# Local attention of a hybrid layer one stage earlier: key sums in global attention, values in the mixing stage, routing at its end

## What is computed

```python
# 1. local attention (windows of 2x2 pixels, 256 windows an image) and a convolutional MLP
q, kv = xw @ wq.T * gq + bq, xw @ wkv.T * gkv + bkv
logit = q_win * SCALE @ k_win.T                 # window means
r_idx = top_k(logit, 4)                         # routing: four windows for each window
k_sel, v_sel = kv[r_idx]                        # 16 keys, 8 heads of 16 channels
x = x + softmax(q * SCALE @ k_sel) @ v_sel + dwconv5x5(v_img, w_lepe) + b_lepe
x = x + fc2(relu(dwconv3x3(fc1(x))))
# 2. global attention over the 1024 tokens of an image, 4 heads of 32 channels
t = t + attention(layernorm(t))
# 3. mixture of experts: 8 experts of 128x128, two chosen for each token
n = layernorm(t); t = t + n + sum_e(combine[:, e] * (gelu(n @ w1[e] + b1[e]) @ w2[e] + b2[e]))
```

## Time and profile before

| | us |
|---|---|
| median of 3 runs | 2374.11 |
| lowest and highest run | 2373.70, 2374.38 |
| the profiled execution's own time | 2376.31 |
| its span, first to last instruction | 2374.8 |

### The profile page before, as it was taken

How to read it: one execution, slowest core, us unless ns; L and a number is a source line. 1 busy time by engine, 2 the same in 40 slices (tenths; PEclk the granted TensorE clock), 3 DMA queues, 4 the chain that set the end, 5 groups by cost and what they waited for, 6 DMA issues and landing times.

```text
span 2374.8 us, 39761 instructions
## 1 busy us (share of the span) xinstructions
PE 1640.0 (69%) x15168; PEld 1067.5 (45%) x15168; DVE 1498.8 (63%) x2500; ACT 940.0 (40%) x1285; POOL 1130.7 (48%) x582
## 2 busy tenths in 40 slices
PE   2006457876687856777568874787667885889897
PEld 1003235644455534545346543564345543555565
DVE  2992686548774486736766378653877548852654
ACT  0001235523464315632256233552245522753682
POOL 1994893248803595046930389114880349600000
PEclk9558768987889878889789897888878987999998
DMA  4102000100002000020000100011000200000000
GB/s 148 45 0 98 10 0 19 58 34 0 10 19 81 10 1 10 19 81 10 10 19 15 68 9 10 19 47 44 0 10 19 72 10 0 10 1 2 10 2 10
DMA packets 26138, 61.75 MB, mean 26 GB/s; under 512 B 4192, under 2 KB 13408, under 8 KB 25824
## 3 DMA queue, kind: packets, MB, share of 16 engines
q0 software_dynamic: 9216, 33.56, 4.1%
q1 hardware_dynamic: 16736, 25.60, 3.3%
HBM read 46.56 MB, written 12.58 MB: 25 GB/s over the span
## 4 chain that ended last, share of the span: by engine, by line
PE 35%; DVE 31%; issue 20%; POOL 7%; ACT 5%; DVEq 1%; SPq 1%; DMA 1%; POOLq 0%; ACTq 0%
PE psB L371 8%; PE psB L487 6%; DVE PROD L921 5%; POOL KV L1253 5%; DVE KVSEL L928 5%; PE psB L452 5%; DVE PT L1123 4%; DVE P L1010 4%; PE psA L538 4%; PE psB L507 3%; DVE STACKED L1110 2%; PE psB L435 2%; POOL KVSEL L1240 2%; PE psB L504 2%; ACT P L675 1%
## 5 line engine op out<-in xcount | busy, mean ns | idle before, releaser
L1271 POOL TENSOR_TENSOR XLEPE<-XLEPE,KVSEL 128x1024 f32<-128x1024 f32 x175 | 430.9, 2462 | 14.6
L1010 DVE CUSTOM_DVE_ANT_0 P<-psB,W 128x1024 f32<-128x1024 f32 x256 | 312.9, 1222 | 132.2 <-PE psB L371 105.1
L1253 POOL TENSOR_TENSOR KV<-KVSEL,Q 128x1024 f32<-128x1024 f32 x112 | 262.1, 2369 | 234.1 <-DVE S L897 189.7
L1240 POOL DMA_INDIRECT KVSEL<-window_table,CHOSEN x64 | 60.9, 952 | 621.1 <-DVEq L968 533.5
L675 ACT ACTIVATE P<-P,NEGMAX 128x1024 f32<-128x1024 f32 x256 | 292.8, 1144 | 157.5 <-DVE NEGMAX L1013 154.9
L487 PE MATMUL psB<-W,P 128*128 128x128 f32 x2048 | 317.8, 305 | 53.1 <-DVE NEGMAX L1010 33.6
L683 ACT ACTIVATE PT<-psB 128x1024 f32<-128x1024 f32 x256 | 260.9, 1019 | 145.6 <-PE psB L487 141.4
L487 PEld LDWEIGHTS psB<-W,P 128*128 128x128 f32 x2048 | 258.7, 155 | 124.8 <-issue 86.1
L371 PE MATMUL psB<-STACKED 96*128 96x512 f32 x512 | 213.2, 502 | 131.9 <-DVE NEGMAX L1010 110.8
L1267 POOL TENSOR_SCALAR KVSEL<-V_PAD,W 128x1024 f32<-128x1024 f32 x175 | 255.3, 1459 | 54.1 <-POOL XLEPE L1271 34.6
L1123 DVE SCALAR_TENSOR_TENSOR PT<-psB,PT 128x128 f32<-128x128 f32 x512 | 137.9, 342 | 218.2 <-PE psB L507 213.4
(11 more groups left out here) (128 smaller groups left out, 2277.1 us busy)
## 6 DMA issues: line engine op xcount, KB each, us to landing
window_table<-KV SPq DMA_DIRECT2D x8, 1024.0 KB, 4.0
X<-x_by_window_dram SPq DMA_DIRECT2D x8, 512.0 KB, 3.5
XLEPE<-x_dram SPq DMA_DIRECT2D x8, 512.0 KB, 3.5
out_dram<-PT SPq DMA_DIRECT2D x8, 512.0 KB, 4.6
W<-packed_dram SPq DMA_DIRECT2D x1, 3714.5 KB, 11.7
KVSEL<-window_table,CHOSEN POOLq DMA_INDIRECT x64, 5.7
FC<-packed_dram SPq DMA_DIRECT2D x8, 64.0 KB, 2.4
PROD<-gains_dram SPq DMA_DIRECT2D x1, 256.0 KB, 12.3
```

Source lines behind the costliest of these rows:

```text
L1010: dve.tensor_tensor_reduce(P[:, b, :], ps[:], w("band", at, at + TOK), 1.0, -3.0e38, ALU.mult, ALU.max, NEGMAX[:, b, 0:1]).then_inc(free, 1)
L1253: pool.tensor_tensor(PRODUCTS[i % 2].rearrange("p (k c) -> p k c", c=C), KVSEL[:, t, keys, 0:C], Q[:, t, q, :].unsqueeze(1).broadcast_to([ ...
L1271: pool.tensor_tensor(acc, acc, product, ALU.add).then_inc(lepe_done, 1)
```

## The change

The local attention is pipelined one stage deeper. `attention(n)` now begins with the residual of image n+1 and then runs the 16 key sums and four softmax steps of image n+2, one at each of 20 of the 31 units. `mixing(n)` runs the 16 value steps of image n+2, ten of them ahead of `accumulate(0)`, and ends with the routing of image n+3. On PE the routing's matmuls leave the attention part of the table for experts 4 to 7, and the transposes of attended values move from the start of the mixing stage to behind experts 1 and 2. The residual writes its sum to TN instead of in place, so that XLEPE is free for the next raster image at once; RT, which had lain in TN, gets its own tile. ACT loses one of seven function table loads an image. SP issues the raster load ahead of the table store. The loop runs over images 0 to 4. Ahead of it, image 1's key sums and softmax run before the first mixing stage, and that stage has its 16 value steps and the routing of image 2.

```diff
@@ -100,12 +102,13 @@
 
 def mixing_order():
 
-    order = [("var", 1, 0), ("wo", 1), ("rstd", 1, 0), ("centred", 1, 1), "image values", ("fc1", 0), ("var", 1, 1), ("fc1", 1),
-             ("rstd", 1, 1), "router", ("dw", 0, 0), ("dw", 0, 1), ("hidden", 0), ("fc1", 2), "start", "combine",
-             ("hidden", 1), ("fc1", 3), ("dw", 1, 0), ("dw", 1, 1)]
+    order = [("var", 1, 0), ("wo", 1), ("fc1", 0), ("rstd", 1, 0), ("centred", 1, 1), ("fc1", 1), ("var", 1, 1),
+             ("dw", 0, 0), ("dw", 0, 1), ("rstd", 1, 1), ("fc1", 2), "router", ("hidden", 0), ("fc1", 3), "start", "combine",
+             ("hidden", 1), ("dw", 1, 0), ("dw", 1, 1)]
     beside = {0: ["fc2"], 1: [("centred", 0, 0), ("centred", 0, 1)], 2: [("var", 0, 0), ("var", 0, 1)],
-              3: [("rstd", 0, 0), ("rstd", 0, 1)], 4: ["v", ("q", 0), ("k", 0)], 5: [("q", 1), ("k", 1)],
-              6: [("q", 2), ("k", 2), ("scores", 0)], 7: [("q", 3), ("k", 3)]}
+              3: [("rstd", 0, 0), ("rstd", 0, 1)], 4: ["windows", "v", ("q", 0), ("k", 0), "logits"],
+              5: [("rows", 0), ("q", 1), ("k", 1), ("rows", 1)],
+              6: [("rows", 2), ("q", 2), ("k", 2), ("rows", 3), ("scores", 0)], 7: ["image values", ("q", 3), ("k", 3)]}
     for e in range(EXPERTS):
         order.append(("expert", e))
...
 
 ORDER_B = main_order()
-RING_B = Ring([(name, m) for m in range(2) for name in ROUTING + ["image values"]]
-              + [(name, 0) for name in ORDER_B if images_ahead(name) == 1], ORDER_B, images_ahead, 3)
+RING_B = Ring([(name, m) for m in range(2) for name in ROUTING + ["image values"]], ORDER_B, images_ahead, 3)
 RING_A = Ring([(("attended", t), 0) for t in range(WTILES)],
               [("pv", c) for c in range(TT)] + [("attended", t) for t in range(WTILES)], images_ahead, 2)
...
-EARLY_STEPS = 28
-EARLY_LINKS = 14
-
-WINDOW_STEPS_AT = [4, 7, 11, 14, 17, 20, 23, 27]
+SCORE_STEPS = 20
+VALUE_LINKS = 22
+
+SCORE_STEPS_AT = [1, 2, 3, 4, 5, 7, 8, 9, 10, 12, 13, 14, 15, 17, 18, 19, 21, 23, 26, 28]
 LINKS_B = 67 - 4 - TT
 LINKS_FIRST = 13
 
...
@@ -226,7 +227,7 @@
         NEGMAX = sb("NEGMAX", [128, P_BUFFERS, 2])
         L = sb("L", [128, TT, HEADS_C])
 
-        RT = TN[:, HALF + 2 * C:HALF + 3 * C]
+        RT = sb("RT", [128, 128])[:]
         ACC = PT[:, GROUPS]
 
...
             def load_raster(m):
                 if not (isinstance(m, int) and m == 0):
-                    sp.wait_ge(x2_ready, 2 * (2 * m - 1))
+                    sp.wait_ge(x1_ready, m)
                 sp.dma_start(XLEPE[:], x[bass.ds(m, 1)].rearrange("a c n -> (a c) n")).then_inc(raster_in, 16)
 
...
                 sp.dma_start(out[bass.ds(n, 1)].rearrange("a (t p) c -> p (a t) c", p=128), ACC).then_inc(out_done, 16)
 
-            def image_traffic(n, first, after):
+            def image_traffic(n, first, third, after):
 
                 if first is not None:
-                    store_table(first)
+                    load_raster(first)
+                if third is not None:
+                    store_table(third)
                 if after is not None:
                     x_is_free(after)
                     load_x(after)
-                if first is not None:
-                    load_raster(first)
                 store_out(n)
 
...
+                if images[2] is not None and name in (("expert", 1), ("expert", 2)):
+                    a_attended(images[2], name[1] - 1)
+
+            def image(n, second, first, third):
 
...
                         exp(u + 1, n)
                     turned(u, n)
-                    if first is not None and ROUTED_AT.get(u) == "windows":
-                        a_windows(first)
+                    if first is not None and u in (SCORE_STEPS_AT[16], SCORE_STEPS_AT[17]):
...
+                if third is not None:
+                    a_values(third)
+                if second is not None:
+                    high(3, second)
 
             act.wait_ge(weights_in, 16 * WEIGHT_DMAS)
...
                 for p in range(PX):
                     hy, wx = divmod(p, 2)
-                    place = XLEPE[:].rearrange("c (j hy i wx) -> c hy j i wx", **dims)[:, hy, 8 * t:8 * t + 8, :, wx]
+                    place, summed = (x[:].rearrange("c (j hy i wx) -> c hy j i wx", **dims)[:, hy, 8 * t:8 * t + 8, :, wx]
+                                     for x in (XLEPE, TN))
                     second_chain(m).mark(dve.scalar_tensor_tensor(
-                        out=place, in0=psA[s][:, p * 128:(p + 1) * 128].rearrange("c (j i) -> c j i", j=8),
+                        out=summed, in0=psA[s][:, p * 128:(p + 1) * 128].rearrange("c (j i) -> c j i", j=8),
                         scalar=col("b_lepe"), in1=place, op0=ALU.add, op1=ALU.add))
...
                 steps = []
                 if second is not None:
-                    later_chain.at_image(second - 1, EARLY_LINKS)
-                    steps = second_half(second)[EARLY_STEPS:]
-                front = first_half(first) if first is not None else []
-                run(front, 1)
+                    later_chain.at_image(second - 1, VALUE_LINKS)
+                    for t in range(WTILES):
+                        window_residual(second, t)
+                if first is not None:
+                    later_chain.at_image(first - 1)
+                    steps = second_half(first)[:SCORE_STEPS]
                 for u in range(1, UNITS):
                     scale_scores(u, n)
...
                 for half in range(2):
                     chain.link(dve.scalar_tensor_tensor(out=XR[:, columns(half)], in0=ps[:, columns(half)], scalar=col("b_fc2"),
-                                                        in1=XLEPE[:, columns(half)], op0=ALU.add, op1=ALU.add))
+                                                        in1=TN[:, columns(half)], op0=ALU.add, op1=ALU.add))
                     dve.sem_inc(x2_ready, 1)
...
                     dve.sem_inc(out_ready, 1)
 
-            def mixing(n, second, first, chain):
-                steps = []
-                if first is not None:
-                    steps = second_half(first)[:EARLY_STEPS]
+            def mixing(n, second, first, third, chain):
+                steps = second_half(first)[SCORE_STEPS:] if first is not None else []
+                front = first_half(third) if third is not None else []
                 if n is not None:
                     spread(1, 0, n)
                     projected(1, n)
-                    if second is not None:
-                        for t in range(WTILES):
-                            window_residual(second, t)
+                    run(steps, 2)
                     normalise(1, 0, n, chain)
                     spread(1, 1, n)
                     dve.tensor_tensor(XR[:, columns(0)], XR[:, columns(0)], LATER_TN[0], ALU.add).then_inc(sum_ready, 1)
+                    run(steps, 2)
                     normalise(1, 1, n, chain)
                     dve.tensor_tensor(XR[:, columns(1)], XR[:, columns(1)], LATER_TN[1], ALU.add).then_inc(sum_ready, 1)
-                if first is not None:
-                    later_chain.at_image(first - 1)
-                run(steps, 2)
-                if n is not None:
+                    run(steps, 2)
                     experts_chosen(n, steps)
                 run(steps, 2)
                 accumulate(0, n)
-                run(steps, 3)
+                run(steps, 2)
                 if second is not None:
                     fc2_residual(second, chain)
-                run(steps, 3)
+                run(steps, 2)
                 accumulate(1, n)
-                run(steps, 3)
+                run(steps, 16)
                 accumulate(2, n)
-                run(steps, 3)
+                run(front, 1)
                 if second is not None:
                     for half in range(2):
                         spread(0, half, second)
                 accumulate(3, n)
-                run(steps, 2)
                 if second is not None:
                     for half in range(2):
                         normalise(0, half, second, chain)
-                run(steps, 2)
                 accumulate(4, n)
                 if second is not None:
                     values(second, chain)
                     low(0, second, chain)
+                run(front, 1)
                 accumulate(5, n)
-                run(steps, 4)
+                run(front, 1)
                 if second is not None:
                     low(1, second, chain)
+                run(front, 1)
                 accumulate(6, n)
-                run(steps, 2)
+                run(front, 1)
                 if second is not None:
                     low(2, second, chain)
+                run(front, 1)
+                if second is not None:
                     scale_scores(0, second)
                 accumulate(7, n)
-                run(steps, 4)
                 if second is not None:
                     low(3, second, chain)
                     chain.check()
```

(16 more changed lines are left out.)

113 lines of the change are left out of this document (58 added, 55 removed).

## The result

| | before | after |
|---|---|---|
| median, us | 2374.24 (4 runs) | 2280.25 (4 runs) |
| lowest and highest run, us | 2373.70, 2377.97 | 2267.83, 2292.22 |
| the profiled execution's own time, us | 2376.31 | 2267.83 |
| its span, us | 2374.8 | 2265.6 |
| mean granted TensorE clock | 0.841 | 0.855 |

The ratio is 0.960, with a 95% interval of 0.955 to 0.966: 94 us faster, where 2291 had been predicted, which is 83 us. The profiled execution of after happens to be its fastest, so its stages sum to 12 us less than the median.

The account below looks back on a forecast made before the run. No engine alone bounds; PE and DVE hand over to each other. Start +55, attention 0 to 5 -91, mixing 0 to 4 -15, mixing 5 -14, attention 6 -18: -83, so 2291 us, range 2220 to 2365.

Parts of the forecast that it names:

- The hole takes the value steps: Mixing ahead of accumulate(0): 38 us of value steps cost 13; mixing's parts become 77, 39 and 48 us.
- Rival A: Mixing: value steps are not hidden, accumulate(0) comes 14 us later than forecast, total 2429 us; chance 0.10.
- Blocking: Mixing ahead of accumulate(0): nine short DVE operations beside POOL's taps lose 8 us, bounds 0 and 25 us.
- the 7.5 us of a pair: Mixing, value steps beside taps: each value pair takes 7.5 us, taken from image 0 before the change.
- Attention: Attention stage: 100 us, bounds 100 and 114; 15 us saved in each of six images, 91 us.
- The term of DVE's busy time: Attention: DVE is busy for 78.3 us, to which 21.9 us of idle time from image 6 are added.
- Waits at the first and third key sum: Attention: DVE waits for POOL at these two sums only, about 7 us, given back by the better fit.
- Mixing: Mixing stage: 165 us against 168.0, saving 15 us over mixing 0 to 4.
- some waits: Mixing: allowance that takes the stage's sum from 164 to 165 us.
- Routing: Last part of mixing: routing adds 18 us, upper end 20.9; mixing 5, without it, loses 16 us to 149.
- The start: Ahead of the loop: key sums and softmax before the first mixing stage put the first attention at 387 us, +55.
- POOL sets the pace (B): Attention: each key sum waits for POOL's product, attention stays at 115 us, total 2381 us; chance 0.12.

Follow-up runs that it names:

- Experiment 4: Against the changed kernel with the choice of experts ahead of all but two value pairs (2209.8 us): all value steps behind accumulate(0); 2394.1 us, ratio 1.009.
- tiny taps: Changed kernel with each of POOL's 25 taps on 64 of its 1024 pixels: 2141.5 us in one execution.
- experiment 7: Changed kernel with its hardware loops written out on all five engines: 2267.3 us, ratio 0.957.
- experiment 1: Changed kernel with two exponentials of image 1's softmax on ACT moved behind the first mixing stage's last convolution evacuation: 2250.3 us, ratio 0.949.
- experiment 8: Changed kernel with exponentials later on ACT, experts' choice first, key sums later: three edits looped 2165.7 us; key sums from unit 3, straight 2098.4, looped 2156.6 us.

## Why the prediction was right, and where it was not

The time and its side held, and 2280 lies well inside 2220 to 2365. By stages of the profiled executions the saving is 121 us in attention of images 0 to 5, 47 in mixing 0 to 4, 11 in mixing 5 and 19 in attention 6, less 93 for the start. By the prediction's own steps:

- **The hole takes the value steps: right, and the gain hangs on it.** 77, 39 and 48 us were predicted for the three parts of mixing, 73.4, 38.6 and 47.2 measured. Experiment 4 shows what stood behind it: with these value steps directly behind the hole a kernel that otherwise takes 2210 us is slower than before. Rival A, by which value steps cost their full length, holds behind `accumulate(0)`, where five pairs cost 37.6 us, and not ahead of it, where they cost 7.1.
- **Blocking: right in kind, near in size.** 8 us predicted, 6.8 counted, 7.2 with L1078. Without these 7.2 us `accumulate(0)` would come at 67. The tiny taps gave 63.8, since the value multiplications lose time as well; that had been in the 7.5 us of a pair.
- **Attention: 100 predicted, 95.2 measured, 93.1 to 94.1 in images 1 to 4.** The term of DVE's busy time was too large: 78.3 against 74.2. 2.4 of it is the residual (L974 at 678.56), which runs ahead of `scale_scores(1)` and so belongs to mixing by the cut that the prediction uses. Most of the rest is that neighbouring rows overlap: sixteen sums were added at 1.22 us each, but the row behind a sum starts some 0.09 us before the sum ends (a sum starts at 692.50 and the scaling behind it at 693.63), which makes 1.3 us in image 2. A sum and a unit, taken as 2.64 us for POOL's pace, follow one another at 2.49 (692.50, 694.99). The idle time was 19.8 where image 6's 21.9 was taken.
- **Waits at the first and third key sum: half right.** The third waits 4.50 us. The first does not in images 1 to 4; experiment 7 shows that the loop's jump hides it, 4.39 us without.
- **Mixing: 165 predicted, 158.5 measured.** On average 2.9 us of it is `accumulate(0)`, 2.6 the two later parts together, and one the "some waits" of the last step. That the last part came out at 47.2 for 48 is luck: 18 of the 48 were routing, which turned out small, next point.
- **Routing: the term that was mis-sized.** 16 us had been taken off for image 5, after 20.9 in the old attention. Mixing 5 took 151.5 (predicted 149) against 158.5 with routing, 7 us. But 5 of these are the jump, which image 5 doesn't have: against image 4, which leaves the loop, routing costs 2.1 us (3.3 in the second profile of the kernel). What filled the last part in place of the 18 us: the jump has 5, routing 3.2 (42.9 in image 4, 39.7 in image 5), and without both it is 39.7 us where image 6 of before had 30.2; that difference was not followed up. Why routing costs so little there is not shown; it may be that its matmuls find room in the ring between experts. In the start, where no experts lie between, the 16 fits: from the last normalisation (381.8) to the first attention are 42.8 us, 42 predicted.
- **The start: the step that failed.** +55 predicted, +92.6 measured (first attention at 387 and at 424.6). The prediction followed POOL and DVE there and let the first mixing stage run in PE's and ACT's shadow. It missed that on ACT two exponentials stand ahead of `fc1`'s copy: experiment 1 gives back 29 us. And it took the first key sum from the earlier trace rows as if nothing ahead of it changed. But the new table also gives the routing products of images 0 and 1 other buffers of the ring, and that sum came 9 us later; this term the prediction put at nothing.
- **POOL sets the pace (B): refuted.** With products of 0.46 us attention falls by 4.5 of 95 us, the length of the wait at the third sum.

That the sum came within 11 us of the median is therefore partly luck: +37 in the start, -61 in the stages of the profiled execution, and 12 between this execution and the median.

## What to carry to other kernels

A wait of one engine is room for another's work only if that work doesn't stand ahead of what the first engine waits for next. Find the hole, then put the short producer of the next link first and the filling behind it; this was worth another 70 us here, after the 94 of the change. When a prologue gets new work, follow every engine's queue through it, above all an engine that does little there: two exponentials of 0.6 us in front of a 1.2 us copy cost 29 us, and a new order of the buffers 9. And before a wait is taken away, ask which other wait it covers: the loop's jump hid a wait for POOL of nearly its own length, so writing the loop out alone gave 10 us. Together with the rest it gave 58, of which over 30 are the unexplained rhythm of experiment 8.

## What the runs showed of the hardware

- A hardware loop's jump costs DVE some 5 us of issue per iteration in this kernel (4.7 to 5.5 us ahead of the first operation of a turn in after, 4.1 to 6.7 over all looped kernels). Straight code has 0.3 us there, and its stages are 5 us shorter from `accumulate(4)` on.
- DVE operations with two SBUF inputs vary with POOL beside them by up to a factor of fourteen (128x64 takes 0.22 us alone, up to 2.39 beside taps and up to 3.11 beside products), and long ones (128x2048) take 2.28 to 4.48. A slowed short one ends 0.07 to 0.09 us behind the end of a POOL operation, and POOL loses time to DVE in turn (2.34 to 4.28 us for an addition). How they meet moves a stage: in two executions of one kernel, after, `accumulate(0)` comes from 70.6 to 77.2 us into mixing, and experiment 8 has 6 us between two kernels with the same operations.
- Executions of after differ by 1% (2268 to 2292), those of the first three of before by 0.03%, although later sets of before spread from 2361 to 2385 as well. A measurement of this kernel does not resolve the 0.2% that the prediction had assumed.
